# A six-stage decoder on one core: where the layer norm's last operation runs, and a new order of the steps

## The reference

```python
x = x + self_attention(LN(x))       # self0: 16 heads of 8, causal mask, softmax
x = x + cross_attention(LN(x), ctx) # cross0: 8 heads of 64, bias on the output
x = x + bit_linear(LN(x))           # ffn: row-wise quantised x, ternary weights
x = x + self_attention(LN(x))       # self1: 16 heads of 8, scores clipped to +-10
x = x + cross_attention(LN(x), ctx) # cross1: 16 heads of 64
x = x + experts(LN(x))              # moe: 8 experts of 128x128, softmax gate,
                                    # gate weights under 0.1 dropped, rest renormalised
```

## Time and profile before

| | |
|---|---|
| median of 3 runs | 502.49 us (502.48 to 504.28) |
| the profiled execution | 503.06 us |
| its span, first to last instruction | 501.3 us |
| outside the span | 1.8 us |
| mean granted TensorE clock in the span | 0.993 of 2.4 GHz |
| busy: PE, ACT, DVE, POOL | 98%, 87%, 80%, 74% |

### The profile page before, as it was taken

One profiled execution on the slowest core, in us unless ns is written; L12 is line 12 of the kernel. 1 busy time (PEld: TensorE's weight loads), 2 busy tenths in 40 slices (PEclk: granted clock), 3 DMA queues, 4 the chain that ended last, 5 costly groups with the idle time before them and its releaser, 6 DMA issues.

```text
span 501.3 us, 15722 instructions
## 1 busy us (share of the span) xinstructions
PE 491.1 (98%) x5516; PEld 418.6 (83%) x5516; DVE 400.8 (80%) x906; ACT 438.0 (87%) x1180; POOL 370.4 (74%) x455
## 2 busy tenths in 40 slices
PE   7999999999999999999999999999999999999995
PEld 4888886878988888888888888888988888888883
DVE  6767778887888898988898898888898687776663
ACT  5889899999898898998898998989889899898761
POOL 2886577887768788869679859986777788477662
PEclk9999999999999999999999999999999999999997
DMA  6800000000000000000000000000000000000000
GB/s 202 325 3 2 3 1 3 1 2 3 2 2 2 7 3 7 2 4 6 7 1 7 2 3 7 3 7 3 8 2 1 9 7 2 7 1 3 7 7 16
DMA packets 6460, 8.64 MB, mean 17 GB/s; under 512 B 1392, under 2 KB 4848, under 8 KB 6384
## 3 DMA queue, kind: packets, MB, share of 16 engines
q1 hardware_dynamic: 5952, 6.86, 4.1%
q10 hardware_dynamic: 432, 0.79, 0.5%
HBM read 6.50 MB, written 1.05 MB: 15 GB/s over the span
## 4 chain that ended last, share of the span: by engine, by line
PE 84%; POOL 5%; ACT 4%; issue 2%; POOLq 1%; DVE 1%; SPq 1%; DMA 1%; DVEq 0%; ACTq 0%
PE psum L1265 13%; PE psum L1252 9%; PE psum L1292 9%; PE psum L1208 8%; PE psum L1330 8%; PE psum L1239 6%; PE psum L1278 3%; PE psum L1460 3%; PE psum L1342 2%; PE psum L1303 2%; PE psum L1305 2%; PE psum L1280 2%; PE psum L1304 2%; POOL w_self L717 2%; POOL w_cross L722 2%
## 5 line engine op out<-in xcount | busy, mean ns | idle before, releaser
L717 POOL TENSOR_TENSOR w_self<-w_self 128x1024 f16<-128x1024 f32 x64 | 120.9, 1897 | 19.3 <-ACT w_self L788 10.0
L722 POOL TENSOR_TENSOR w_cross<-w_cross,e_rec_cross 128x1024 f32<-128x1024 f32 x48 | 90.8, 1897 | 24.3 <-DVE e_rec_cross L984 24.3
L799 ACT ACTIVATE w_cross<-psum,row_max_cross 128x128 f32<-128x128 f32 x384 | 104.6, 407 | 4.5 <-DVE row_max_cross L975 4.1
L975 DVE TENSOR_REDUCE row_max_cross<-psum 128x8 f32<-128x1024 f32 x48 | 58.0, 1216 | 14.4 <-PE psum L1252 13.9
L982 DVE TENSOR_REDUCE e_sum_cross<-w_cross 128x8 f32<-128x1024 f32 x48 | 58.2, 1212 | 5.3 <-ACT w_cross L799 5.0
L807 ACT ACTIVATE w_cross<-psum 128x1024 f32<-128x1024 f32 x48 | 50.1, 1043 | 5.1 <-PE psum L1265 5.1
L1252 PE MATMUL psum<-kT_cross,qT_cross 64*128 64x128 f32 x768 | 54.2, 283 | 0.0
L1292 PEld LDWEIGHTS psum<-w_cross,v_cross 128*64 128x64 f32 x768 | 41.1, 136 | 14.9 <-issue 12.4
L1252 PEld LDWEIGHTS psum<-kT_cross,qT_cross 64*128 64x128 f32 x768 | 46.2, 187 | 6.8 <-issue 5.1
L1292 PE MATMUL psum<-w_cross,v_cross 128*64 128x128 f32 x768 | 51.4, 278 | 0.4 <-ACT w_cross L807 0.4
L1265 PE MATMUL psum<-ident,w_cross 128*128 128x128 f32 x384 | 49.9, 273 | 0.5 <-POOL w_cross L722 0.5
(11 more groups left out here) (212 smaller groups left out, 1380.9 us busy)
## 6 DMA issues: line engine op xcount, KB each, us to landing
out_dram<-x_all SPq DMA_DIRECT2D x16, 64.0 KB, 1.6
x_all<-in_x SPq DMA_DIRECT2D x1, 768.0 KB, 7.6
cT_all<-in_ctx SPq DMA_DIRECT2D x1, 768.0 KB, 9.5
e_k<-in_e_k SPq DMA_DIRECT2D x1, 512.0 KB, 5.3
e_v<-in_e_v SPq DMA_DIRECT2D x1, 512.0 KB, 6.1
e_q<-in_e_q SPq DMA_DIRECT2D x1, 512.0 KB, 8.3
e_o<-in_e_o SPq DMA_DIRECT2D x1, 512.0 KB, 10.4
m_w<-in_m_w SPq DMA_DIRECT2D x1, 512.0 KB, 8.2
```

Source lines behind the costliest of these rows:

```text
L717: pool.tensor_tensor(L.w_low[u], L.w[u][:], halves(L.w[u][:]), ALU.subtract)\
L722: pool.tensor_tensor(L.diff[u][:].rearrange("p (h k) -> p h k", h=UNIT), L.e[u][:].rearrange("p (h k) -> p h k", h=UNIT), L.e_rec[:, u, :] ...
L799: last = act.activation(L.e[u][:, P * p:P * (p + 1)], S_[:, P * p:P * (p + 1)], ACT.Exp, bias=L.row_max[:, u, p:p + 1])
L975: dve.tensor_reduce(L.row_max[:, u, :], group(i, turn)[:].rearrange("p (h k) -> p h k", h=UNIT), AX_X, ALU.max, negate=True).then_inc(L.ma ...
```

## The change

GpSimd's step `L.rs` keeps its first operation (the power) and gets another second one: instead of the 128x1 `minus_mean` it writes the 128x128 `xn = (x - mean) * rstd` itself, in one TENSOR_SCALAR with two operations. ScalarE's step `L.nm` and the tile `minus_mean` are gone. The waits that `L.nm` had, for the former sequence's transpose (or, for ffn, for its quantised units), are now GpSimd's, between the power and the second operation. DVE's `stats` of the next sequence now waits for `xn` rather than for `minus_mean`. The two norms that were done otherwise stay as they are.

```diff
                 if (L, i) in ((self0, 0), (moe, NSEQ - 1)):
                     power.then_inc(L.rstd_ready, 1)
                     return
+                if i and L is not ffn:
+                    pool.wait_ge(x_full, full(i - 1, f"{L.name}.xT"))
+                if i and L is ffn:
+                    pool.wait_ge(units_ready, i)
                 pool.drain()
-                pool.tensor_scalar(L.minus_mean[:], L.mean_var[:, 0:1], L.rstd[:], -1.0, ALU.mult, ALU.mult)\
-                    .then_inc(L.rstd_ready, 1)
+                pool.tensor_scalar(L.xn[:], x_all[:, i, :], L.mean_var[:, 0:1], L.rstd[:], ALU.subtract, ALU.mult)\
+                    .then_inc(L.xn_ready, 1)
...
-            def normalise(L, i):
-                act.wait_ge(L.rstd_ready, i + 1)
-                if i and L is not ffn:
-                    act.wait_ge(x_full, full(i - 1, f"{L.name}.xT"))
-                if i and L is ffn:
-                    act.wait_ge(units_ready, i)
-                act.activation(L.xn[:], x_all[:, i, :], ACT.Identity, bias=L.minus_mean[:], scale=L.rstd[:])\
-                    .then_inc(L.xn_ready, 1)
...
             def stats(L, i, x):
                 if i:
-                    dve.wait_ge(L.rstd_ready, i)
+                    dve.wait_ge(L.xn_ready, i)
```

```diff
                 if step == "g":
...
                     if i == NSEQ - 1:
-                        keep_busy(bank(i, name), 2)
+                        keep_busy(bank(i, name), 1)
...
                 if step == "gT":
+                    room(i, name)
+                    if i == NSEQ - 1:
+                        keep_busy(bank(i, name), 4)
                     pe.wait_ge(*emptied(i, "moe.g"))
-                    room(i, name)
                     pe.transpose(bank(i, name)[:, 0:P], g_weight[:], ident[:]).then_inc(x_full, 1)
...
                 if step == "xT":
                     room(i, name)
-                    if L is moe and i == NSEQ - 1:
-                        keep_busy(bank(i, name), 4)
...
-                act.activation(weighted[:, e, :], group(NSEQ - 1, "moe.e")[:, P * e:P * (e + 1)], ACT.Copy,
+                act.activation(cross1.attnT[:, e, :], group(NSEQ - 1, "moe.e")[:, P * e:P * (e + 1)], ACT.Copy,
                                    scale=g_mix[:, e:e + 1]).then_inc(parts_ready, 1)
```

The table `ORDER` is replaced as a whole, and with it the order on all four engines; one line of it and one of the assumed costs:

```diff
-        add(f"{L}.rs", "POOL", 940, [source], [f"{L}.nm"], first=580 if L == "self0" else None,
-            last=580 if L == "moe" else None)
+        add(f"{L}.rs", "POOL", 1150, [source], [f"{L}.un" if L == "ffn" else f"{L}.xT"],
+            first=900 if L == "self0" else None, last=580 if L == "moe" else None)
...
-        "aHaJa4a4aOa4a4aLaHa6a6a6aQaJbqa6aUbWbWbWbYbYaXaObYb2b2b0aUaLaZbYaHaQb0aJb0b0a1a6aXaOaLbaa4aHbcaZaJaQ"
+        "aGaIa3a3aKaNa3a5aGa3a5aPa5aTaIa5bUbobSbSbSbUaWaNbYaKbYbWaGbUaTbUaIaPa5bWbWaYbWa0aWaNa8a3aKaGbaaYaIaP"
```

More of the change, by code:

```diff
@@ L60, in but_last, with ago_but_last @@
     return name, lambda i: i if i < NSEQ - 1 else None
+def ago_but_last(name):
+    return name, lambda i: i - 1 if 0 < i < NSEQ - 1 else None
 def last_only(name):
@@ L87, in norm @@
     def norm(L, source, users, read="xTe"):
-        add(f"{L}.rs", "POOL", 940, [source], [f"{L}.nm"], first=580 if L == "self0" else None,
-            last=580 if L == "moe" else None)
-        add(f"{L}.nm", "ACT", 380, [but_last(f"{L}.rs") if L == "moe" else f"{L}.rs", source],
-            [f"{L}.un" if L == "ffn" else f"{L}.xT"], first=300 if L == "self0" else None, last=170 if L == "moe" else None)
+        add(f"{L}.rs", "POOL", 1150, [source], [f"{L}.un" if L == "ffn" else f"{L}.xT"],
+            first=900 if L == "self0" else None, last=580 if L == "moe" else None)
         if L == "ffn":
-            add(f"{L}.qz", "DVE", 760, [f"{L}.nm"], [f"{L}.res"])
+            add(f"{L}.qz", "DVE", 760, [f"{L}.rs"], [f"{L}.res"])
             add(f"{L}.un", "ACT", 287, [f"{L}.qz"], [f"{L}.xT"])
-        made = dict(ffn=["ffn.un"], moe=[but_last("moe.nm"), last_only(source)]).get(L, [f"{L}.nm"])
+        made = dict(ffn=["ffn.un"], moe=[but_last("moe.rs"), last_only(source)]).get(L, [f"{L}.rs"])
         fill(f"{L}.xT", 109, made, f"{L}.{read}", users)
-        add(f"{L}.xTe", *(("DVE", 250) if L == "ffn" else ("ACT", 332 if L == "moe" else 166)), [f"{L}.xT"])
+        add(f"{L}.xTe", *(("DVE", 250) if L == "ffn" else ("ACT", 332 if L == "moe" else 166)),
+            [f"{L}.xT"])
     def self_attention(L, source, maxima, following, loads, loads_out):
@@ L181, in all_steps @@
     fill("moe.g", 124, ["moe.xTe", "in.moe"], "moe.w")
-    add("moe.e", "PE", 1385, ["moe.xl", "m_w.lo"], ["moe.sm"], "S", "moe.ml")
+    add("moe.e", "PE", 1385, ["moe.xl", "m_w.lo"], (), "S", "moe.ml")
     add("moe.lg", "DVE", 300, ["moe.g", last_only("moe.rs")])
@@ L187, in all_steps @@
     add("moe.gTe", "ACT", 167, ["moe.gT", last_only("moe.e")], last=1150)
-    add("moe.ml", "DVE", 1150, ["moe.e", "moe.w", last_only("moe.nm")], ["moe.o"], last=1600)
+    add("moe.ml", "DVE", 1150, ["moe.e", "moe.w", last_only("moe.xTe")], [ago_but_last("moe.o")], last=1650)
     add("moe.sm", "POOL", 3293, ["moe.ml"], ["moe.o"], last=0)
-    fill("moe.b", 223, ["moe.gTe"], "moe.o", last=330)
+    fill("moe.b", 223, ["moe.gTe"], "moe.o", last=560)
     add("moe.o", "DVE", 198, ["moe.b", "moe.sm"])
@@ L847, in do_step @@
                     high_copy(name.partition(".")[0])
-                if step == "nm" and L is moe and i == NSEQ - 1:
-                    keep_last()
-                elif step == "nm" and (L, i) != (self0, 0):
-                    normalise(L, i)
                 if step == "un":
@@ L862, in do_step @@
                     if L is moe:
+                        if i == NSEQ - 1:
+                            keep_last()
                         moe_parts(i)
@@ L914, in do_step @@
                     if i == NSEQ - 1:
-                        act.wait_ge(emptied(i - 1, "moe.b")[0], emptied(i - 1, "moe.b")[1])
                         act.wait_ge(mix_ready, 1)
@@ L1046, in gate_logits @@
                 if i == NSEQ - 1:
-                    dve.wait_ge(moe.rstd_ready, NSEQ)
+                    dve.wait_ge(moe.rstd_ready, 1)
                     dve.scalar_tensor_tensor(out=logits[:], in0=bank(i, "moe.g")[:, 0:EXPERTS], scalar=moe.rstd[:],
@@ L1098, in finish @@
                 dve.wait_ge(x_full, full(i, "moe.b"))
-                dve.tensor_tensor(x_all[:, i, :], bank(i, "moe.b")[:, 0:P], mix, ALU.add)\
+                dve.tensor_tensor(x_all[:, i, :], bank(i, "moe.b")[:, 0:P], mix if i < NSEQ - 1 else moe.xn[:], ALU.add)\
                     .then_inc(emptied(i, "moe.b")[0], 1)
@@ L1439, in moe_step @@
                         pe.wait_ge(parts_ready, n + 1)
-                        last = pe.matmul(out_, ident[:], weighted[:, e, :], start=n == 0, stop=n == 3)
+                        last = pe.matmul(out_, ident[:], cross1.attnT[:, e, :], start=n == 0, stop=n == 3)
                     last.then_inc(x_full, 1)
```

94 lines of the change are left out of this document (45 added, 49 removed).

## The result

| | before | changed |
|---|---|---|
| median | 502.49 us (4 runs, 502.37 to 504.28) | 509.87 us (4 runs, 508.86 to 510.72) |
| the profiled execution, its span | 503.06, 501.3 us | 509.21, 507.5 us |
| the last output projection of sequence 15 starts | 486.2 us | 495.4 us |
| from there to the end of the span | 15.15 us | 12.11 us |
| norm's second operation on GpSimd | 264 ns | 798 ns |

The recorded ratio of the executions is 1.0161, 95% interval 1.0126 to 1.0197; the quotient of the two medians is 1.0147, inside it. The forecast was 498.7 with a range up to 501.7. The rows of the last output projection and of the stretch behind it, read from the timelines, split the 6.2 us between the two spans: 9.2 us more ahead of the last output projection, 3.04 us less behind it.

A forecast was written before the change was run, and what follows sets the result against it. PE's own work was taken as the bound. Gains of 0.5 + 0.3 + 3.1 = 3.9 us gave 499.2 profiled, 498.6 as median, stated as 498.7 us; own range 497.5 to 500.0, 8-in-10 range 496.8 to 501.7.

The forecast's parts named there:

- The price of the operation: GpSimd's new norm operation: 0.45 us each, between 264 and 458 ns, adding 0.19 us each, 18 us in all.
- Both ScalarE and GpSimd stay 20 points under PE: Middle: ACT about 78%, GpSimd 77%, so 49 us removed and 18 us added do not reach the end as such.
- rival 4: Middle: slower, 505.5 us, as norms on GpSimd delay what follows, perhaps longer by meeting VectorE in SBUF; chance 0.05.
- rival 3: Middle: 2 to 3 us worse, 501.3 us, as GpSimd's queue is held waiting for the former transpose; chance 0.12.
- The list of waits: PE's waits in the middle: 1.9 us in all, so nobody keeps PE waiting for long.
- The order: PE's new step table: waits could change 1.5 us either way, counted as nothing; fewer shape changes counted separately.
- The 0.3 us for three changes of shape fewer: PE's new order: 187 changes of array shape instead of 190, about 0.09 us each, 0.3 us gained.
- The relief of ScalarE: Middle: PE's 0.2 us wait, a share of a 0.7 us wait and a shorter norm, 0.5 us gained.
- The end, 3.1 us: Last sequence: experts' products start 2.1 us earlier, last sum about 496.0 instead of 499.06; 3.1 us if the clock holds.
- Rival 1: End of last sequence: the clock falls early, so only 1.6 us less, 500.9 us; chance 0.2.
- the signs set beforehand: GpSimd's operations 0.3 to 0.47 us, ScalarE busy 385 to 392 us, PE standing 1 to 3.5 us between 20 and 485.
- The one meant for GpSimd: Sign in PE's waits: forecast wrong if those for GpSimd's `w_self` or `w_cross` sum to more than 2 us.

The follow-up runs named there:

- with one column: Kernels with the new end, no self/cross wait for the former transpose, and GpSimd writing one column of xn: 501.09 us in the old order, 503.68 in the new.
- the new end: Kernel before, with ScalarE's norm and its order, given only the changed kernel's steps after the last output projection: 500.46 us, ratio 0.9963.
- that appended stretch: Changed kernel with ten forms of GpSimd's elementwise operation appended behind its last step, three times each; some 20 us longer, only the operations were timed.
- the first group: Executions of the unchanged kernel before, run beside the first four timed follow-up kernels: median 502.30 us.
- the first one-column kernel: Changed kernel, but GpSimd's norm operation writes only the first of 128 columns of xn: 503.64 us, ratio 1.0028.

## Why the prediction was wrong

In the order of its steps; each size is a difference of the medians above, unless a trace is named.

- **The price of the operation.** "I use 0.45, near the upper end", with 458 ns as the bound above: it is 798. The bound was taken from a two-input operation, on the thought that one tensor less can't cost more; the form with scalars costs more than that in every variant measured (533 to 796 on 128 columns against 455). This is the first failed step. It puts 94 x 0.53 = 50 us on GpSimd in place of 18, and costs 6.8 us from 381 to 798 ns (7.5 in the middle of the traces). The Trainium skill, GPSIMD Engine Reference, section "Engine selection", calls one-input work on GpSimd roughly line-rate, which would put it under two-input work; here the measurement decides, and it is the other way round.
- **"Both ScalarE and GpSimd stay 20 points under PE, so neither the 49 us nor the 18 us reach the end as such."** The second failed step, and it would have failed at 0.45 too. A share of the span says nothing of how late a result may be. GpSimd's slack took up the first 0.2 us per norm and then let the rest through, with GpSimd busy 83%. That is rival 4 (given 0.05), but for its contention with VectorE, which the 797 to 801 ns do not show: I had worked out that 0.07 us of every norm must reach PE to lose 6.4 us, and 6.8 / 94 = 0.07 us is what arrived. The wait for the former transpose (rival 3) cost nothing. The list of waits, on which I leaned, also counts too little: between 20 and 480 us of the new order PE stands 7.5 us with 128 columns and 3.1 with one, 4.4 more, where the middle is 7.5 us longer; the modelled ends of matmuls may hide the rest.
- **The order, "and I put nothing".** The new table is 1.7 us worse at an equal clock, and 2.6 in medians. I had read the waits of the middle in the old order and had no way to read the new one from that trace. The 0.3 us for three changes of shape fewer shows nowhere: the middle of the traces is 0.1 to 0.2 us longer. Where it loses is read from the traces: with one column it is 0.8 us behind at the 61st of PE's 737 steps and 0.95 at the last output projection. At the 61st step the five traces of the old order with no fall of the clock in the start-up stand at 47.57 to 48.24 us, and the six of the new one at 48.81 to 50.33. So most of it is the start-up; what in the start-up was not tried.
- **The relief of ScalarE, 0.5 us.** Nothing, and perhaps 0.3 the other way. The reading of the earlier trace rows that nobody waits for ScalarE's `xn` was right, and its conclusion should have been zero. The 49 us were wrong too: ScalarE's busy time fell by 32.5, to 405.5, where I had 385 to 392.
- **The end, 3.1 us.** The mechanism came out, and every point of its chain within 0.4 us (12.11 us for 15.15). The size was off because a new end at full clock was set against an old one in which the clock had fallen to half. In 18 of 29 executions of the kernel before the mean clock is as low as in that one, but in 6 of 12 it is low with the new end too; between medians the gain is 1.85 us, and at an equal clock 1.1 to 1.7. Rival 1, an early fall, fits two of the four executions of the changed kernel (510.6 us at a mean clock of 0.997, beside 509.0 at 0.999 and 1.00), at a cost of 1.6. Where it fell in those two no trace shows; in three traces of the same order it fell at the experts' products.

The sum, by medians: 502.3 - 1.85 (end) + 0.25 (ScalarE's operations gone) + 0.4 (381 for 264 ns) + 2.6 (order) + 6.75 (381 to 798 ns) - 0.6 (the wait, so no cost) = 509.9. It adds up because each term is the step from one measured kernel to the next, so the total proves nothing; 0.6 of it may be the groups of runs. At a mean clock of 0.999 or 1.00 the same steps are 500.74 - 1.10 + 0.51 + 0.51 + 1.72 + 7.63 - 0.98 = 509.03 (11 to 2 executions each). Had the operation taken the 0.45 us that I assumed, the forecast would still have been 5 us too low: between the measured 503.64 at 381 ns and 504.44 at 584 ns the time would have been about 503.9, an estimate. Of the signs set beforehand, three showed the failure: 798 ns for 0.3 to 0.47 us, ScalarE's busy time, and PE standing 7.4 us between 20 and 485 us for 1 to 3.5. The one meant for GpSimd, over 2 us of waits for `w_self` and `w_cross`, did not: they sum to 1.4 us, beside 3.2 for GpSimd's `xn`.

## What to carry to other kernels

When work moves to another engine, bound its price there from the same form of instruction (operations, kinds of scalar), not from one that looks dearer; the nearest row here was the wrong kind and low by 340 ns. Ask first what the freed engine was holding up: if PE hardly waits for it, the move has little to gain, and a kernel in which the operation is simply left out tells it in one run. An engine at 75% is not a place for free work if a result that another engine needs stands behind each piece of it; and a gain at the end of a kernel should be counted over several executions at both clocks, since one profile shows only one of them. Between two orders, the distance between two steps with the same work ahead of them, read from each trace, leaves out the start-up and the end, in which executions of one kernel differ.

## What the hardware showed that I had not expected

- GpSimd on 128 fp32 columns: TENSOR_TENSOR 455 ns with two tensors, 400 where the second is one column spread out; TENSOR_SCALAR 533 with an immediate, 602 with one scalar from SBUF, 648 with two operations and immediates, 796 with two operations and two scalars from SBUF. The two-operation form on a single column takes 398 in that appended stretch and 380 to 385 in the norm.
- Its duration hardly varies: 797 to 801 ns over all 94, with VectorE busy 79% beside it, and 796 with VectorE idle.
- With the same instructions the clock falls in some executions and not in others: the mean is 0.997 or less in 49 of 75 of the kernel before (in the first group 2 us slower) and in 6 of 12 with the new end (1.5 us). The mean does not tell where. In six of the traces it fell at the experts' products of the last sequence, behind PE's stands there; but it also fell at 18 us, behind a stand of 1.67 us, and at 108 us, behind one of 1.84. So a stand may cost more than its length; only the one at the end was tested. With three dummy products where PE had stood 0.84 us there the mean was 0.999 or 1.00 in 12 of 12. In the profiled execution of the first one-column kernel (new order, with the wait), in which it fell, the windows of the end are these (us, PE busy, PEld, DVE, ACT, POOL, granted clock, DMA share, GB/s):

```profile
491.00:495.00 4.00, 2.70 (x10) 1.95 (x11) 2.39 (x11) 0.92 (x5) 2.79 (x4) 0.90 0.00 0
495.00:498.00 3.00, 2.67 (x8) 1.07 (x7) 1.70 (x5) 0.92 (x4) 0.12 (x1) 0.57 0.00 0
498.00:501.70 3.70, 1.38 (x10) 1.19 (x10) 0.29 (x1) 0.50 (x2) 0.00 (x0) 0.91 0.12 35
```

It was 1.00 up to 491, fell in the stretch in which PE stands for `moe_lo` and the experts' products begin, and was mostly back in the last window.
